# A token stage on one NeuronCore: sixteen transposes of the next tile, in four groups of four or singly between the products

## What is computed

```python
x = x + tanh(g_xattn) * attend(layernorm(x), ctx)            # scores -> softmax -> mix of ctx rows
h = layernorm(x)
query  = h @ Wq.T                                             # 64 wide
scores = (query @ Wr.T) @ (aux_keys @ Wr.T).T / sqrt(48) + log_rel
top8   = top_k(scores, 8)
w      = softmax(query . aux_keys[top8] / 8 + log_rel[top8])
aux    = (w @ aux_values[top8]) @ Wvd.T @ Wvu.T
u      = f(var(h), gelu(h @ Wu1.T + bu1) @ Wu2.T + bu2)       # Wu1: 512 x 2048
x = x + tanh(g_ffn) * (h + sigmoid-gate(u) * aux)
```

## Time and profile before

| | |
|---|---|
| median of 3 runs | 1263.33 us (1262.03 to 1266.67) |
| profiled execution, from its first to its last instruction (span) | 1260.6 us |
| mean granted TensorE clock over the span | 0.973 |
| busy: TensorE matmuls, TensorE weight loads | 1196.1 us, 1063.0 us |
| busy: VectorE, ScalarE, GpSimd | 748.7 us, 460.8 us, 188.3 us |
| transposes into the token stage's banks | 512, 272 ns each as shown |

### The profile page before, as it was taken

How to read it: one execution, slowest core, us unless ns; L and a number is a source line. 1 busy time by engine, 2 the same in 40 slices (tenths; PEclk the granted TensorE clock), 3 DMA queues, 4 the chain that set the end, 5 groups by cost and what they waited for, 6 DMA issues and landing times. The chain is left out here.

```text
span 1260.6 us, 21177 instructions
## 1 busy us (share of the span) xinstructions
PE 1196.1 (95%) x7402; PEld 1063.0 (84%) x7402; DVE 748.7 (59%) x1886; ACT 460.8 (37%) x747; POOL 188.3 (15%) x276
## 2 busy tenths in 40 slices
PE   7999797998999999999999999999999948999998
PEld 6999787977999999999999999999999934555554
DVE  6555754456156566666665666666666565665564
ACT  3333333344033343334333434343434246333332
POOL 0000500000012222222222222222222144000000
PEclk9999888999999999999999999999999968999999
DMA  7333369777184312301113101132111136888884
GB/s 267 134 133 137 97 199 308 243 256 233 37 221 132 104 65 72 110 36 64 36 64 118 64 36 62 38 103 79 63 37 63 38 101 267 313 319 333 331 327 174
DMA packets 114327, 183.17 MB, mean 145 GB/s; under 512 B 45813, under 2 KB 94997, under 8 KB 97561
## 3 DMA queue, kind: packets, MB, share of 16 engines
q1 hardware_dynamic: 109112, 145.02, 35.1%
q10 hardware_dynamic: 4608, 33.56, 6.6%
q0 software_dynamic: 576, 4.19, 0.8%
HBM read 138.45 MB, written 54.79 MB: 153 GB/s over the span
## 5 line engine op out<-in xcount | busy, mean ns | idle before, releaser
L46 PE MATMUL tk_hidden_sum<-b_weights,k_turned 128*128 128x384 f32 x512 | 180.0, 351 | 0.0
L48 PE MATMUL tk_hidden_sum<-b_weights,k_turned 128*128 128x384 f32 x512 | 172.2, 336 | 0.0
L47 PE MATMUL tk_hidden_sum<-b_weights,k_turned 128*128 128x384 f32 x512 | 171.2, 334 | 0.0
L46 PE MATMUL tk_b_sum<-b_weights,k_turned 128*128 128x320 f32 (+1 forms) x528 | 169.9, 322 | 0.0
L48 PE MATMUL tk_b_sum<-b_weights,k_turned 128*128 128x320 f32 (+1 forms) x528 | 163.9, 310 | 0.0
L47 PE MATMUL tk_b_sum<-b_weights,k_turned 128*128 128x320 f32 (+1 forms) x528 | 163.7, 310 | 0.0
L962 ACT ACTIVATE k_turned<-tk_bank 128x512 fp32r<-128x512 f32 x128 | 76.4, 598 | 202.5 <-PE tk_bank L76 184.6
L1132 DVE TENSOR_TENSOR k_turned<-tk_bank,k_turned 128x512 fp32r<-128x512 f32 x128 | 88.3, 691 | 65.6 <-ACT k_turned L962 65.1
L46 PEld LDWEIGHTS tk_b_sum<-b_weights,k_turned 128*128 128x128 f32 x528 | 99.3, 188 | 6.1 <-issue 5.9
L47 PEld LDWEIGHTS tk_b_sum<-b_weights,k_turned 128*128 128x128 f32 x528 | 99.4, 188 | 0.0
L48 PEld LDWEIGHTS tk_b_sum<-b_weights,k_turned 128*128 128x128 f32 x528 | 99.1, 188 | 0.0
(11 more groups left out here) (262 smaller groups left out, 2648.0 us busy)
## 6 DMA issues: line engine op xcount, KB each, us to landing
k_rows<-in_x_dram SPq DMA_DIRECT2D x54, 1024.0 KB, 4.9
out_dram<-k_rows ACTq DMA_DIRECT2D x22, 1024.0 KB, 5.0
k_rows<-in_Wk_dram SPq DMA_DIRECT2D x16, 1024.0 KB, 4.7
k_rows<-in_Wq_dram SPq DMA_DIRECT2D x16, 1024.0 KB, 6.1
ob_x<-in_x_dram SPq DMA_DIRECT2D x10, 1024.0 KB, 6.5
out_dram<-ob_x ACTq DMA_DIRECT2D x10, 1024.0 KB, 5.2
b_weights<-scratch_b SPq DMA_DIRECT2D x6, 1024.0 KB, 6.7
scratch_mt<-k_way_out SPq DMA_DIRECT2D x32, 128.0 KB, 2.2
```

The costliest lines, as they stand in the source:

```text
L46: pe.matmul(out, lh, rh, start=start, stop=False, skip_group_check=skip)
L47: pe.matmul(out, lh, rl, start=False, stop=False, skip_group_check=skip)
L48: return pe.matmul(out, ll, rh, start=False, stop=stop, skip_group_check=skip)
```

## The change

`a_part` gets a parameter `turning`. Where it is true, each slice's three products are followed by one transpose of a slice of the next tile, into the same bank and columns as before; the first of them carries the wait for the bank (and for `centred`, in group 0), the last one signals `turned`. The four calls of `turn_x` in `tile` are gone; those ahead of the loop stay.

```diff
--- before.py
+++ after.py
@@ -831,13 +831,22 @@
                                         (bw[0][:, c, :], bw[1][:, c, :]), c == 0, c == KC - 1, True)
                 return ins
 
-            def a_part(t, u, g, first):
+            def a_part(t, u, g, first, turning=True):
 
                 if g == 0 and not first:
                     pe.wait_ge(S["hidden"], t)
-                for c in range(4 * g, 4 * g + 4):
+                for k in range(4):
+                    c = 4 * g + k
                     split_product(pe, psA[:, 0:UB], (xT[u][0][:, c, :], xT[u][1][:, c, :]),
                                   (wu[0][:, c, :], wu[1][:, c, :]), c == 0, c == KC - 1, True)
+                    if turning:
+                        if k == 0:
+                            if g == 0:
+                                pe.wait_ge(S["centred"], t + 2)
+                            pe.wait_ge(S["x_lo"], G * (t + 1) + g - 1)
+                        ins = pe.transpose(bank[g % 2][:, k * P:(k + 1) * P], x[1 - u][:, c * P:(c + 1) * P], ident[:])
+                if turning:
+                    ins.then_inc(S["turned"], 1)
 
             def late_query(t, first=False):
                 pe.wait_ge(S["query"], t + 1)
@@ -882,25 +891,16 @@
                 b_part(t, u, 3).then_inc(S["b_sum"], 1)
                 if late:
                     late_route(t - 1, late_first)
-                a_part(t, u, 0, first)
-                if not last:
-                    pe.wait_ge(S["centred"], t + 2)
-                    turn_x(t + 1, 1 - u, 0)
-                a_part(t, u, 1, first)
-                if not last:
-                    turn_x(t + 1, 1 - u, 1)
+                a_part(t, u, 0, first, not last)
+                a_part(t, u, 1, first, not last)
                 pe.wait_ge(S["att"], t + 1)
                 if first:
                     pe.wait_ge(S["cw_scaled"], 2)
                 pe.transpose(att_turned_ps, att2[u], ident[:]).then_inc(S["att_turned"], 1)
-                a_part(t, u, 2, first)
-                if not last:
-                    turn_x(t + 1, 1 - u, 2)
+                a_part(t, u, 2, first, not last)
                 if late:
                     late_turn_w(t - 1)
-                a_part(t, u, 3, first)
-                if not last:
-                    turn_x(t + 1, 1 - u, 3)
+                a_part(t, u, 3, first, not last)
                 if late:
                     late_z(t - 1)
```

## The result

The kernel before takes 1263.09 us (median of 14 runs), the changed one 1267.07 us (14 runs); the ratio is 1.0026, with a 95% interval of 1.0014 to 1.0037. The medians lie 4.0 us apart and the means 3.3 us, which is what the ratio gives: 3.3 us slower, 1.8 to 4.7 us, and within the 0.5% that count as no change here. The forecast was 1266.5 us, in a range from 1261.5 to 1275.

The account below looks back on a forecast made before the run. TensorE, never idle in the token stage, was taken as the bound, its time the sum of instruction costs. Profiled span 1260.6 us plus 3.2 for lone transposes, plus 2.7 from span to median, gave 1266.5 us; range 1261.5 to 1275.

Parts of the forecast that it names:

- Rival B: Token stage, ahead of group 2: PE stalls through the moved wait; 0.3 us a tile would be +9.3 us; chance 0.05.
- the three prices: Lone transpose between products, read at three places: 0.110, 0.117 or 0.139 us; the forecast took the second, 0.117.
- L846 (0.110): One transpose between 320-column products: costs 0.110 us, 0.002 more than now, +0.7 us over 372.
- L895 in the last tile (0.139): Transpose standing alone in the last tile: costs 0.139 us, 0.031 more than now, +11.5 us.
- 372 x 0.0085 = 3.2 us: Token stage: 372 moved transposes, each costing 0.0085 us more alone between products than in a row.
- Why nothing is gained: Token-stage transposes: too short to hide the load that follows; spreading changes which load is exposed, not how many.
- Rival C: Token stage: lone transposes are hidden and cost 0.060 us, saving 25 us, to 1238 us; chance 0.07.
- Rival A: Products behind each lone transpose run slow too: 11.5 us in full, 1274.8 us, deciding from 0.125 us each; chance 0.11.
- Rival D: No difference that can be seen: lone transposes at L846's price, +0.7 us, 1264.0 us; chance 0.22.

Follow-up runs that it names:

- the second measurement: The changed kernel run once more, unaltered, against the kernel before: ratio 1.0017 (1.0001 to 1.0033) over 10 runs; period 21.093 us a tile.
- group_half_load: Kernel before, with the second and third transpose of each group loading 64 columns of weights instead of 128: 21.027 us a tile.
- row_bf16: Kernel before, with the second and third of each four transposes in a row made bf16: 20.646 us a tile.
- the common floor: Changed kernel with only the last transpose of each group left, twelve of a tile's sixteen dropped: 19.748 us a tile.
- lone_bf16: Changed kernel, with the second and third transpose of each group turning the upper halves of the fp32 values as bf16: 21.195 us a tile.
- half_moving: Changed kernel, with the second and third transpose of each group streaming 64 columns (64 rows of x) instead of 128: 23.354 us a tile.
- half_load: Changed kernel, with the second and third transpose of each group loading 64 columns of weights instead of 128: 21.040 us a tile.

## Why the prediction was right, and where not

**Right: what bounds the stage, and that the waits cost nothing.** PE has no idle time in the stage after, and the bank was free 0.90 to 1.08 us ahead of need, where 0.84 to 1.02 was read from before. Rival B had no ground.

**Right: the choice among the three prices.** The cycle of a lone transpose was put at 0.637 us from the last transpose of a group, and the mean is 0.6369. L846 (0.110) was a little too low, L895 in the last tile (0.139) far too high. That the slow products behind L895 belong to that place and not to being alone was right: in the changed kernel they are gone, there too.

**Partly wrong: the sum.** 372 x 0.0085 = 3.2 us was right for what it counted. By stretches of the tile, the four a_parts with their transposes grew by 0.079 us; the slow stretch behind L895, 0.022, was lost in them, so the places cost 0.101, or 0.0084 each. But 0.022 went back there, and another 0.0125 in products that have no moved neighbour, the b_parts and the context products (6 ns each, unexplained). 0.067 us a tile is left, 2.1 us, not 3.2. The step that missed is the one that multiplied a price by a count, and left the neighbours as they were. The total came out at 3.3 us all the same (1.8 to 4.7; the second measurement has 2.1, 0.1 to 4.2), and that this meets the forecast's 3.2 is luck. Between the token stage's 2.1 us and that there may be a late clock in the output stage in more runs of one kernel than of the other, or nothing at all: in the second measurement the clocks are alike, and the offset at equal clock is 2.1 us.

**Wrong: the mechanism in "Why nothing is gained".** It said that in a row each transpose costs the next one's load, and that spreading them changes which load is exposed. Halving these loads changed nothing (group_half_load, 21.027), and, but for at most 0.006 us, an fp32 load fits behind a bf16 transpose of 0.056 us (row_bf16). What is left as the row's limit is the fp32 stream itself. The conclusion stood for another reason: the loads were not exposed in the row before, so there was nothing for the products to hide, and the stream is paid in either order (0.107 and 0.112 us). The prediction read two rows that stood 0.11 us apart as loads, where they were streams; both readings give 0.11, and no row of the trace before tells them apart.

The Trainium skill, page "TensorE: Matmul & The Clock Gate", section "LDWEIGHTS (loading the stationary operand)", has a load of 128 columns at 107 ns. The prediction took 0.1085 us in a row as agreement. The runs speak against it: behind a bf16 transpose, the next fp32 one started after 0.056 us and cost 0.006 more than elsewhere, so of that load at most 0.006 us showed beyond the stream ahead of it. By the formula of its section "Back-to-back issue gap", matmuls of 128 columns start 56 ns apart. The bf16 transposes agree (0.056, 0.057), the fp32 ones, at 0.107, don't. The same section has some 81 ns for streams of load and matmul pairs, which neither of them meets.

Rival C lived on that reading of the loads, and is dead with it. Rival A's price of 0.125 us was reached by no fp32 transpose; a lone bf16 one does cost it, but with a load of its own that isn't hidden, which is not what A had in mind. Rival D's 0.110 us, from the narrower products, was 0.002 too low by the common floor.

## What to carry to other kernels

Before spreading short instructions between long ones to hide their loads, shorten the load alone in one run: if the time stays, there is nothing to hide. In this stage the engine was never idle, and a reordering moved the time by nanoseconds per place: a lone transpose cost 5% more than one in a row. Where a stage repeats, take the distance of one instruction over thirty repeats; it showed 0.007 us a tile, where the spread of whole runs is 6 us.

## What the runs showed of the hardware that was not expected

- At the 2.4 GHz level, an fp32 128x128 transpose takes TensorE 0.107 us in a row, and halving its load changes nothing (group_half_load); a bf16 one takes 0.056 (row_bf16).
- Alone between 384-column fp32r products, the bf16 one costs 0.125 us, more than the fp32 one's 0.112. The fp32 one's weights are loaded behind the product ahead, the bf16 one's (operands at a step of two) start loading only with the transpose, 240 times of 240 (lone_bf16).
- A transpose that uses 64 rows of the array between products that use 128 adds 0.28 us over a full one, two and a half times the full one's price (half_moving); its load, too, starts only with the transpose. One that uses 128 rows and 64 columns of weights adds nothing (half_load).
- A late rise of the clock after a pause goes with 4 us: the output stage took 216.4 us where it came 5.5 us behind the first product, and 220.4 where it came 14.3 us behind.
